# Last layer of a four-layer image kernel: row-by-row copy of the turned banks, one gelu instruction per channel group

## Chip, core and metric

One NeuronCore of one Trainium2 chip runs the whole program. The metric is the device time of one execution in microseconds (us), lower being better. The kernel before took 12187.03 us, the median of three runs (12183.24 to 12192.82).

## The reference, cut to what matters

Four layers run one after the other on x of shape (4, 48, 256, 256), each as x + layer(groupnorm(x)), all in float32. Only the last one is touched:

```python
y = jnp.einsum('oc,bchw->bohw', w_in, x)            # 48 -> 288 channels
yp = y as 8x8 patches
f = jnp.fft.rfft2(yp) * fft_mask[None]
y = irfft2(f), patches put back
y = depthwise 3x3 conv of y, padding 1
x1, x2 = jnp.split(y, 2, axis=1)                    # 144 channels each
g = jax.nn.gelu(x1, approximate=False) * x2
return jnp.einsum('oc,bchw->bohw', w_out, g)        # 144 -> 48 channels
```

## The kernel before, in words

`stage_l3` is the last layer. It works in N = 66 slabs: 33 bands of eight image rows, once for the images 0 and 2 and once for 1 and 3. Every engine has its own instruction stream, written out by hand, and semaphores join them. `n` is the slab, `j` one of three channel groups (24 channels of x1 and the 24 of x2 that belong to them), and `u = 3 n + j` counts the groups.

The steps, with the engine that does each, are these.

- **Mixing** (`channels`, matmul L2255). TensorE multiplies the 32 patch columns with the input weights, in twelve groups: eight of 3 columns and four of 2. Group 0 to 11 go in turn through four pairs of PSUM banks. Of each pair ScalarE (ACT) copies one bank and VectorE (DVE) the other to the tile `y` (`read_y`, L2389 on ACT, L2373 on DVE). From group 4 on, TensorE waits until the group four places ahead has been read by both.
- **Convolution** (`convolve`, matmul L2298). For each channel one matrix takes the 64 pixels of a patch to 10 x 10 places: mask, transforms and 3x3 filter in one. The 24 channels go in five bank groups (5, 5, 5, 5, 4 channels); ACT copies x1 and DVE x2 to the tile `turn` (`read_turn`, L2389 and L2383). `CONV_SLOTS` says which bank pair each group takes.
- **Edges.** The outer ring of the 10 x 10 places belongs to neighbours. SP moves two edge columns by DMA (`move_edges`, L2203), GpSimd (POOL) adds them (L2528), then adds the strip kept from the band above (L2534, it posts `carried`), and keeps a new strip (L2538).
- **Gelu** (ACT, L2396) in place on the x1 part of `turn`, in two halves of four of the eight columns, 768 elements a lane each. **Gate** (`gated`, DVE, L2472): gelu(x1) times x2, in two halves, each behind its own gelu half.
- **Turning** (`transpose`, L2320). TensorE transposes the gated tile into four banks: two behind the first gate half, two behind the second. `TURN_SLOTS` names the banks.
- **Copy of the turned banks** (`read_rows`, ACT, L2389): four copies of 512 elements a lane to the tile `rows`, each once its bank is turned.
- **Projection** (`project`, L2334) with the output weights for all three groups, then DVE adds the residual (`residual`, L2480, it posts `f_out`) and SP stores.

TensorE's order in one slab is: convolution of group 0, turning of group 2 of the slab before, convolution of group 1, projection of the slab before, turning of group 0, convolution of group 2, mixing for the next slab, turning of group 1. Three of its waits matter here. In the convolution of group 2 the bank groups 0 and 1 wait for the second and the fourth residual, and bank group 2 waits for all four copies of the turned banks of group 0. In the convolutions of groups 0 and 1 the fourth bank group waits until ACT and DVE have read the first. `load_x` (SP, L2187) loads the next slab's input once TensorE has finished mixing: 384 KB a half, into the one tile `x`.

ACT and DVE take their work in the order of the code. ACT before, in one slab:

```python
for g in range(COMP):
    read_turn(act, copy, 0, n, 0, g, a_done, a_out)
    if g in (0, 2) and not first:
        gelu(u - 1, g // 2)
...
for g in range(YR):
    read_y(act, copy, 0, n + 1, g, False, a_done, b_done, a_out)
    if g in (3, 6):
        gelu(u + 1, g // 6)
```

DVE has its gate halves at the same places one group later: after groups 1 and 3 of the convolution, and after groups 4 and 7 of the mixing. "The seventh copy" below is DVE's copy of mixing group 6, "the eighth" that of group 7.

Of the kernel before, what the change touches and what calls it, by code (L numbers as in the profile page):

```python
# [13 lines left out]
ACT = mybir.ActivationFunctionType  # L14
# [2081 lines left out]
def stage_l3(nc, D, S):  # L2096

    C3 = 3 * C
    TX, PX = W // 8, 64
    BANDS = H // 8 + 1  # L2100
    N = 2 * BANDS
# [11 lines left out]
    with nc.cleanup_on_exit(), ExitStack() as ctx:  # L2113
        def sb(name, shape):
            return ctx.enter_context(nc.sbuf_tensor(f"l3_{name}", shape, F32))
# [4 lines left out]
        def sem(name):  # L2120
            return nc.alloc_semaphore(f"l3_{name}")
        d = sb("d", [128, C3, PPOS])
        y = sb("y", [128, C3, 2 * TX])
        turn = sb("turn", [128, 2, 10, 10, 2, CH])
# [4 lines left out]
        rows = sb("rows", [128, 3, GROUPS, 2, 2 * TX])  # L2129
# [16 lines left out]
        t_done, t_out, p_done, f_out = sem("t_done"), sem("t_out"), sem("p_done"), sem("f_out")  # L2146
        edged, carried, saved, mixing, blank = (sem(n) for n in ("edged", "carried", "saved", "mixing", "blank"))
        parted, ended_edge = sem("parted"), sem("ended_edge")
        gelu_out, gate_out = sem("gelu_out"), sem("gate_out")
# [6 lines left out]
        def turn_banks(j):  # L2156

            return [bank for slot in TURN_SLOTS[j] for bank in slots[slot]]

        def half(u, part, h):  # L2160

            return turn[:, u % 2, 1:9, 4 * h:4 * h + 4, part, :]

        def gated_half(u, h):

            return gate[:, u % 2, 32 * h:32 * h + 32, 0:CH].rearrange("p (x y) i -> p x y i", y=4)

        def slabs(work):

            for q in range(2):  # L2170
                for ty in range(BANDS):
                    n = q * BANDS + ty
                    work(q, ty, n, n == 0, n == N - 1)
# [192 lines left out]
        def read_y(eng, copy, s, n, g, first, done, other, ready):  # L2366

            if g == 0 and not first:
                eng.wait_ge(other, n * AB)
            eng.wait_ge(done, n * AB + (g + 1))  # L2370
            bank = slots[MIX_SLOTS[g % 4]][s]
            patches = y[:].rearrange("p c (t s) -> p c t s", s=2)[:, :, STARTS[g]:STARTS[g] + SIZES[g], s]
            copy(patches, bank[:, 0:SIZES[g] * C3].rearrange("p (t c) -> p c t", c=C3)).then_inc(ready, 1)  # L2373
# [12 lines left out]
        @block.scalar  # L2386
        def _(act):
            def copy(o, i):
                return nc.scalar.activation(o, i, ACT.Copy)  # L2389

            def gelu(u, h):

                if h == 0:
                    act.wait_ge(edged, u + 1)
                    act.wait_ge(carried, u + 1)
                nc.scalar.activation(half(u, 0, h), half(u, 0, h), ACT.Gelu).then_inc(gelu_out, 1)  # L2396

            def read_rows(n, j):

                u = n * 3 + j  # L2400
                if j == 0 and n > 0:
                    act.wait_ge(p_done, n * 4)
                for i, bank in enumerate(turn_banks(j)):
                    act.wait_ge(t_done, u * 4 + i + 1)
                    copy(rows[:, j, 4 * i:4 * i + 4].rearrange("p q r (s t) -> p (q r) t s", s=2),
                         bank[:].rearrange("p (q t s) -> p q t s", t=TX, s=2)).then_inc(t_out, 1)
            act.wait_ge(blank, 2)
            for g in range(YR):
                read_y(act, copy, 0, 0, g, True, a_done, b_done, a_out)

            def slab(q, ty, n, first, last):
                u = n * 3
                for g in range(COMP):
                    read_turn(act, copy, 0, n, 0, g, a_done, a_out)
                    if g in (0, 2) and not first:
                        gelu(u - 1, g // 2)
                if not first:
                    read_rows(n - 1, 2)
                for g in range(COMP):
                    read_turn(act, copy, 0, n, 1, g, a_done, a_out)  # L2420
                for h in range(2):
                    gelu(u, h)
                read_rows(n, 0)
                for g in range(COMP):
                    read_turn(act, copy, 0, n, 2, g, a_done, a_out)
                if last:
                    for h in range(2):
                        gelu(u + 1, h)
                else:
                    for g in range(YR):  # L2430
                        read_y(act, copy, 0, n + 1, g, False, a_done, b_done, a_out)
                        if g in (3, 6):
                            gelu(u + 1, g // 6)
                read_rows(n, 1)
            slabs(slab)
            for h in range(2):
                gelu(N * 3 - 1, h)
            read_rows(N - 1, 2)

        @block.vector  # L2440
        def _(dve):
            nc.vector.memset(lt, 0.0).then_inc(cleared, 1)
            dve.wait_ge(cleared, 1)
            for q in range(2):
                for s in range(2):
                    b = q + 2 * s
                    nc.vector.tensor_scalar(lt[:, q, s * HI:s * HI + C], S["k_ident"][0:C, 0:C], S["gn"][0:C, b, 0:1], None,
                                            ALU.mult)
                    last = nc.vector.tensor_copy(lt[:, q, s * HI + C:s * HI + C + 1], S["gn"][0:C, b, 1:2])
            last.then_inc(prep, 1)  # L2450
            nc.vector.memset(out[:], 0.0)
            nc.vector.memset(edge[:], 0.0)
            nc.vector.memset(gate[:], 0.0)
            dve.wait_ge(wy_done, 1)
            for q in range(2):
                last = nc.vector.tensor_copy(wy[:, q, :], e[q][0:HI + C + 1, 0:C6])
            last.then_inc(wy_out, 1)
            dve.wait_ge(wy_out, 1)
            for k in range(4):
                last = nc.vector.memset(e[k][32:HI, :], 0.0)  # L2460
            last.then_inc(blank, 1)
            dve.wait_ge(blank, 1)
            dve.sem_inc(blank, 1)
            for g in range(YR):
                read_y(dve, nc.vector.tensor_copy, 1, 0, g, True, b_done, a_done, b_out)

            def gated(u, h):

                dve.wait_ge(gelu_out, u * 2 + h + 1)
                if u >= 2:  # L2470
                    dve.wait_ge(t_done, u * 4 - 6 + 2 * h)
                nc.vector.tensor_tensor(gated_half(u, h), half(u, 0, h), half(u, 1, h), ALU.mult).then_inc(gate_out, 1)  # L2472

            def residual(n, m):

                dve.wait_ge(p_done, n * 4 + m + 1)
                if m == 0:
                    dve.wait_ge(res_loaded, n * 64 + 64)
                o = out[:, m].rearrange("p s (t x) -> p (s t) x", x=8)
                nc.vector.tensor_tensor(o, e[m][0:HI + C, :].rearrange("p (x t) -> p t x", x=8), o, ALU.add)\  # L2480
                    .then_inc(f_out, 1)

            def slab(q, ty, n, first, last):
                u = n * 3
                for g in range(COMP):
                    read_turn(dve, nc.vector.tensor_copy, 1, n, 0, g, b_done, b_out)
                    if g in (1, 3) and not first:
                        gated(u - 1, g // 2)
                for g in range(COMP):
                    read_turn(dve, nc.vector.tensor_copy, 1, n, 1, g, b_done, b_out)  # L2490
                for h in range(2):
                    gated(u, h)
                if not first:
                    for m in range(4):
                        residual(n - 1, m)
                for g in range(COMP):
                    read_turn(dve, nc.vector.tensor_copy, 1, n, 2, g, b_done, b_out)
                if last:
                    for h in range(2):
                        gated(u + 1, h)  # L2500
                else:
                    for g in range(YR):
                        read_y(dve, nc.vector.tensor_copy, 1, n + 1, g, False, b_done, a_done, b_out)
                        if g in (4, 7):
                            gated(u + 1, g // 7)
            slabs(slab)
            for h in range(2):
                gated(N * 3 - 1, h)
            for m in range(4):
                residual(N - 1, m)  # L2510
# [79 lines left out]
```

## Time and profile before

| | |
|---|---|
| median of three runs | 12187.03 us |
| the profiled execution, its own time | 12192.53 us |
| its span, first to last instruction | 12190.5 us |
| mean granted TensorE clock | 0.978 |
| busy in the whole span: PE / DVE / ACT / POOL | 94% / 58% / 45% / 40% |
| last layer | from 9444 us to the end, 66 slabs |
| 9480 to 12150 us (2670 us): PE busy | 2287.07 us |
| the same: ACT, DVE, POOL busy | 2010.65, 1636.81, 1173.94 us |

A slab takes about 40 us. The 2 us between the profiled execution's own time and its span lie ahead of the first and behind the last instruction. A row of a timeline gives start and duration in us; "idle before" is what the engine waited just ahead, and "issue" stands for a wait that no semaphore of the profile explains. Where several neighbouring instructions of a kind are merged, their number follows an x.

### The profile page before, as it was taken

The page shows a single profiled execution, that of the slowest core. Times are in us where ns is not written, and L with a number is a line of the kernel's source. Part 1 is how long each engine was busy: PE and PEld are TensorE (multiplying, and loading weights), DVE is VectorE, ACT ScalarE, POOL GpSimd, SP SyncE. Part 2 cuts the span into 40 slices and gives each one's busy share as a digit, 9 for nine tenths or more (in the row PEclk, how much of TensorE's full clock was granted, in tenths as well). Part 3 has the DMA queues.
Part 4 walks back from the last instruction along what each step waited for, and adds up shares of the span by engine and source line. Part 5 has one row for each costly group of instructions (what it writes and reads, how often), then busy time and mean ns, then how long its engine had stood idle before and what let it go on. Part 6 is the DMA issues. An engine that isn't in the chain of part 4 may idle for free. (4 is left out here: it accounts for less than half of the span.)

```text
span 12190.5 us, 377334 instructions
## 1 busy us (share of the span) xinstructions
PE 11481.4 (94%) x157286; PEld 8021.8 (66%) x157286; DVE 7085.2 (58%) x16108; ACT 5452.4 (45%) x10670; POOL 4928.3 (40%) x4166
## 2 busy tenths in 40 slices
PE   8999999899989999899999999999999888888888
PEld 7877444399977777555555555555555676676776
DVE  0000355544435544688888888888887665666665
ACT  0000111143433333355555555555554777777776
POOL 0000222211430045566666666666665444444444
PEclk9999999999999999899999999999999999999999
DMA  4333466696894488766666666666665443343443
GB/s 141 132 131 134 126 159 157 149 170 103 152 170 146 137 214 229 111 88 88 88 88 88 89 89 87 89 89 87 88 88 81 105 101 91 95 100 94 98 94 88
DMA packets 2340706, 1418.36 MB, mean 116 GB/s; under 512 B 1877404, under 2 KB 2250395, under 8 KB 2253487
## 3 DMA queue, kind: packets, MB, share of 16 engines
q1 hardware_dynamic: 2064428, 1296.69, 53.9%
q10 hardware_dynamic: 275072, 105.14, 3.7%
q8 instruction: 812, 13.30, 0.5%
q14 instruction: 394, 3.23, 0.1%
HBM read 648.90 MB, written 450.45 MB: 90 GB/s over the span
## 5 line engine op out<-in xcount | busy, mean ns | idle before, releaser
L1795 PE MATMUL l_m<-l_wa,l_pix 128*128 128x288 f32 x8192 | 2211.2, 413 | 2.7 <-DVE l_wb L1977 2.7
L1795 PEld LDWEIGHTS l_m<-l_wa,l_pix 128*128 128x128 f32 x8192 | 1475.3, 190 | 688.5 <-issue 361.5
L1651 POOL TENSOR_TENSOR l_qkv<-l_qkv,l_copies 128x576 f32<-128x576 f32 x1024 | 1438.4, 1405 | 630.6 <-DVE l_qkv L1988 617.0
L1641 POOL TENSOR_TENSOR l_pix<-l_raw 128x516 f32<-128x516 f32 x1024 | 1218.6, 1190 | 1042.3 <-DVE l_t L2025 1017.3
L1476 PE MATMUL l1h_ps<-l1h_ring,l1h_w 96*96 96x256 f32 x6120 | 1326.2, 379 | 62.8 <-ACT l1h_ring L1418 59.2
L1476 PEld LDWEIGHTS l1h_ps<-l1h_ring,l1h_w 96*96 96x96 f32 x6120 | 998.4, 163 | 390.4 <-issue 59.4
L1509 DVE SCALAR_TENSOR_TENSOR l1h_ring<-l1h_ps,l1h_bias,l1h_columns 96x256 f32<-96x256 f32 x1020 | 671.1, 658 | 676.3 <-PE l1h_ps L1476 670.6
L509 PE MATMUL l0a_rows<-l0a_x 128*49 128x245 f32 x8144 | 1043.9, 371 | 0.0
L870 PE MATMUL l0b_bank<-l0b_x,l0b_w 49*64 49x512 f32 x9216 | 1001.3, 593 | 4.4 <-DVE l0b_w L896 4.4
L1890 ACT ACTIVATE l_ks<-l_f 94x384 f32<-94x384 f32 x1024 | 498.7, 487 | 838.2 <-PE l_f L1810 838.2
L1810 PE MATMUL l_f<-l_qkv,l_a 64*94 64x384 f32 x4096 | 835.7, 484 | 1.6 <-POOL l_qkv L1651 1.5
L870 PEld LDWEIGHTS l0b_bank<-l0b_x,l0b_w 49*64 49x64 f32 x9216 | 439.2, 133 | 563.6 <-issue 563.6
L1801 PE MATMUL l_m<-l_wb,l_left 58*128 58x288 f32 x4096 | 774.1, 455 | 0.0
L1460 POOL TENSOR_TENSOR l1h_columns<-l1h_blocks,l1h_ring 96x2048 f32<-96x2048 f32 x63 | 350.8, 5590 | 1033.4 <-DVE l1h_ring L1509 1033.4
L1895 ACT ACTIVATE l_sd<-l_mv,l_eps 128x4 f32<-128x4 f32 x512 | 152.2, 297 | 1289.2 <-DVE l_mv L2008 1289.2
L1901 ACT ACTIVATE l_y<-l_i,l_shift,l_rsd 128x96 f32<-128x96 f32 x2048 | 711.1, 427 | 14.2 <-DVE l_shift L2015 0.6
L1224 PE MATMUL l1v_ps<-l1v_ring_w,l1v_w 48*48 48x130 f32 x20480 | 632.0, 272 | 45.4 <-ACT l1v_ring_w L1147 41.2
L509 PEld LDWEIGHTS l0a_rows<-l0a_x 128*49 128x49 f32 x8144 | 601.8, 124 | 107.5 <-issue 1.4
L2298 PE MATMUL l_a<-l_d,l_y 64*64 64x100 f32 x10296 | 570.5, 255 | 89.6 <-ACT l_rows L2389 35.0
L2383 DVE COPY l_turn<-l_b 128x500 f32<-128x500 f32 (+1 forms) x528 | 351.7, 666 | 505.7 <-PE l_b L2298 502.7
L1224 PE MATMUL l1v_ps<-l1v_ring_p,l1v_w 48*48 48x128 f32 x20320 | 615.1, 269 | 7.3 <-issue 6.9
L1224 PEld LDWEIGHTS l1v_ps<-l1v_ring_w,l1v_w 48*48 48x48 f32 x20480 | 586.4, 120 | 48.6 <-issue 48.5
(272 smaller groups left out, 22474.9 us busy)
## 6 DMA issues: line engine op xcount, KB each, us to landing
l0a_x<-x_px_dram SPq DMA_DIRECT2D x128, 1176.0 KB, 5.1
l_edge<-l_turn SPq DMA_DIRECT2D x396, 236.2 KB
l0b_x<-x_in_dram SPq DMA_DIRECT2D x128, 493.8 KB
l_raw<-l_raw SPq DMA_DIRECT2D x128, 483.6 KB, 7.3
l_raw<-x_dram SPq DMA_DIRECT2D x1270, 48.0 KB, 3.7
l_x<-x3p_dram SPq DMA_DIRECT2D x132, 384.0 KB
l_out<-x_dram SPq DMA_DIRECT2D x264, 192.0 KB, 4.4
out_dram<-l_out SPq DMA_DIRECT2D x132, 384.0 KB, 4.6
```

The source lines that it names most:

```text
L509: last = nc.tensor.matmul(o[odd * ODD:odd * ODD + C1, lo:lo + n * C1], x[:, ks, ys, 2 + odd, :], x[:, k, y, e0 + odd:e0 + odd + n, :].rear ...
L870: last = nc.tensor.matmul(bank[2 * n + rt][h * HI:(h + 1) * HI, :], w[part, t, :], rows(part, k, 4 * n + h + t // 3 - rt)[:, :, t % 3:t % ...
L1224: last = nc.tensor.matmul(ps[g][side(c), r, 0:width], w[side(r), t, :], x, start=(t == 0), stop=(t == TAPS - 1), skip_group_check=True)
L1476: last = nc.tensor.matmul(ps[g][0:C2, 0:GI * V], w[:, kernel, s, :], ring[:, g, before % DEEP, :, s:s + V], start=(s == 0), stop=(s == 2))
L1509: nc.vector.scalar_tensor_tensor(out=ring[:, g, x % DEEP, :, 1:V + 1], in0=ps[g][0:C2, 0:GI * V].rearrange("p (i v) -> p i v", i=GI), scal ...
L1641: nc.gpsimd.tensor_tensor(pix[:, n % 2, i, half * HALF:(half + 1) * HALF].rearrange("p (r w) -> p r w", w=PW), in0, in1, op).then_inc(pix_ ...
L1651: nc.gpsimd.tensor_tensor(q, q, copies[:, g % 2, 1:2, :].broadcast_to([128, 2, OUTC]), ALU.add)\
L1795: last = nc.tensor.matmul(bank[i][:, 0:OUTC], pix[:, k, i, first:first + 128], wa[:, b, i, :], start=True, stop=(i in (1, 2)))
L1801: nc.tensor.matmul(bank[i][:, 0:OUTC], left[rows, k, first:first + 128], wb[rows, b, :], start=False, stop=True).then_inc(conv_done, 1)
L1810: last = nc.tensor.matmul(f[0:SLOTS, h, 0:2 * QK].rearrange("p (n o) -> p n o", n=2), a[k, 0:SLOTS], qkv[k, j % 4, 2 * r:2 * r + 2, 0:QK], ...
L1901: last = nc.scalar.activation(y[:, g, m, :], iv[:, m * C2:(m + 1) * C2], ACT.Identity, scale=rsd[:, g, m:m + 1], bias=shift[:, g, m:m + 1])
L2298: last = nc.tensor.matmul(bank[part * 64:(part + 1) * 64, i * PPOS:(i + 1) * PPOS], y[rows_of, c, :], d[rows_of, c, :], start=True, stop=True,
```

## The change

1. `read_rows` copies a turned bank in the order of its destination. Before, the innermost loop took the two values s = 0, 1, which are neighbours in PSUM, and wrote them 32 elements apart. Now the innermost loop takes the 32 values of t, which lie two elements apart in PSUM, and writes them side by side. Source, destination and values are the same.
2. `gelu` does a group's 8 x 8 x 24 elements in one instruction, behind the same two waits, and posts `gelu_out` once. Both gate halves wait for that one.
3. The places: ACT's gelu of group 2 stands after bank group 1 of the next slab's convolution (before: halves after 0 and 2), that of group 1 after mixing group 4 (before: 3 and 6). DVE's gate halves stand after bank groups 2 and 3 (before: 1 and 3), and after mixing groups 6 and 8 (before: 4 and 7). Gelu and gate of group 0 stay where they were.

```diff
             def copy(o, i):
                 return nc.scalar.activation(o, i, ACT.Copy)
 
-            def gelu(u, h):
-
-                if h == 0:
-                    act.wait_ge(edged, u + 1)
-                    act.wait_ge(carried, u + 1)
-                nc.scalar.activation(half(u, 0, h), half(u, 0, h), ACT.Gelu).then_inc(gelu_out, 1)
+            def gelu(u):
+
+                act.wait_ge(edged, u + 1)
+                act.wait_ge(carried, u + 1)
+                kept = turn[:, u % 2, 1:9, 0:8, 0, :]
+                nc.scalar.activation(kept, kept, ACT.Gelu).then_inc(gelu_out, 1)
...
-                    copy(rows[:, j, 4 * i:4 * i + 4].rearrange("p q r (s t) -> p (q r) t s", s=2),
-                         bank[:].rearrange("p (q t s) -> p q t s", t=TX, s=2)).then_inc(t_out, 1)
+                    copy(rows[:, j, 4 * i:4 * i + 4].rearrange("p q r (s t) -> p (q r) s t", s=2),
+                         bank[:].rearrange("p (q t s) -> p q s t", t=TX, s=2)).then_inc(t_out, 1)
...
                     read_turn(act, copy, 0, n, 0, g, a_done, a_out)
-                    if g in (0, 2) and not first:
-                        gelu(u - 1, g // 2)
+                    if g == 1 and not first:
+                        gelu(u - 1)
...
-                for h in range(2):
-                    gelu(u, h)
+                gelu(u)
                 read_rows(n, 0)
...
                 if last:
-                    for h in range(2):
-                        gelu(u + 1, h)
+                    gelu(u + 1)
                 else:
                     for g in range(YR):
                         read_y(act, copy, 0, n + 1, g, False, a_done, b_done, a_out)
-                        if g in (3, 6):
-                            gelu(u + 1, g // 6)
+                        if g == 4:
+                            gelu(u + 1)
                 read_rows(n, 1)
             slabs(slab)
-            for h in range(2):
-                gelu(N * 3 - 1, h)
+            gelu(N * 3 - 1)
             read_rows(N - 1, 2)
...
             def gated(u, h):
 
-                dve.wait_ge(gelu_out, u * 2 + h + 1)
+                dve.wait_ge(gelu_out, u + 1)
...
                     read_turn(dve, nc.vector.tensor_copy, 1, n, 0, g, b_done, b_out)
-                    if g in (1, 3) and not first:
-                        gated(u - 1, g // 2)
+                    if g in (2, 3) and not first:
+                        gated(u - 1, g - 2)
...
                         read_y(dve, nc.vector.tensor_copy, 1, n + 1, g, False, b_done, a_done, b_out)
-                        if g in (4, 7):
-                            gated(u + 1, g // 7)
+                        if g in (6, 8):
+                            gated(u + 1, g // 8)
```

## Rows read from the trace of the kernel before

**Rows 1.** Waits of TensorE, 9480 to 12150 us: total us, times, longest.

```profile
PE l_e L2298 <- issue: 110.6, 48, 4.6
PE l_e L2255 <- issue: 46.3, 46, 2.6
PE l_a L2298 <- ACT l_rows L2389: 34.6, 63, 0.9
PE l_a L2298 <- ACT l_turn L2389: 27.2, 77, 0.5
PE l_e L2320 <- ACT l_y L2389: 26.1, 37, 1.4
...
PE l_a L2320 <- DVE l_gate L2472: 18.4, 30, 1.5
```

**Rows 2.** Chain of waits in one slab, 10940 to 10982 us: start, us, what.

```profile
10944.29 0.85 ACT l_turn L2396
...
10945.17 0.97 DVE l_gate L2472
...
10947.00 2.43 ACT l_rows L2389 x3
...
10949.73 1.16 ACT l_rows L2389
...
10969.93 1.85 issue
```

**Rows 3.** Last layer, groups of instructions kept apart by shape: busy us, mean ns.

```profile
L2396 ACT ACTIVATE l_turn<-l_turn 128x768 f32<-128x768 f32 x396 | 324.3, 835 | 194.9 <-POOL l_turn L2534 192.8 <-POOLq L2531 2.1
...
L2389 ACT ACTIVATE l_rows<-l_b 128x512 f32<-128x512 f32 x264 | 300.6, 1139 | 0.0
...
L2389 ACT ACTIVATE l_turn<-l_a 128x400 f32<-128x400 f32 x66 | 33.3, 505 | 18.4 <-PE l_a L2298 18.3
```

**Rows 4.** The same slab, timeline of TensorE's weight loads: start, us.

```profile
10948.25 0.89 PEld L2298 LDWEIGHTS l_e<-l_d,l_y 64*64 64x64 f32 x40 [0.27 <-DVE l_out L2480]
10949.44 0.89 PEld L2298 LDWEIGHTS l_e<-l_d,l_y 64*64 64x64 f32 x40 [0.30 <-DVE l_out L2480]
10950.93 0.13 PEld L2298 LDWEIGHTS l_a<-l_d,l_y 64*64 64x64 f32 x1 [0.59 <-ACT l_rows L2389]
```

**Rows 5.** Chain of waits in two other slabs: the long wait after a load.

```profile
10885.32 3.70 issue
...
11048.00 4.06 issue
```

**Rows 6.** Timeline of SP: first half of the input load, three slabs.

```profile
10880.47 0.31 SPq L2187 DMA_DIRECT2D l_x<-x3p_dram  x1
...
10963.79 0.31 SPq L2187 DMA_DIRECT2D l_x<-x3p_dram  x1
...
11043.91 0.31 SPq L2187 DMA_DIRECT2D l_x<-x3p_dram  x1
```

**Rows 7.** Timeline of DVE while two slabs are mixed.

```profile
10960.94 0.73 DVE L2373 COPY l_y<-l_b 128x432 f32<-128x432 f32 x1 [0.30 <-PE l_b L2255]
10961.67 0.70 DVE L2373 COPY l_y<-l_e 128x432 f32<-128x432 f32 x1
10962.26 1.32 DVE L2472 TENSOR_TENSOR l_gate<-l_turn 128x768 f32<-128x768 f32 x1
...
10998.35 1.24 DVE L2373 COPY l_y<-l_b 128x432 f32<-128x432 f32 x2
10999.46 0.73 DVE L2373 COPY l_y<-l_e 128x432 f32<-128x432 f32 x1
11000.07 2.71 DVE L2472 TENSOR_TENSOR l_gate<-l_turn 128x768 f32<-128x768 f32 x1
```

**Rows 8.** Timeline of POOL in the same two slabs: the edge add.

```profile
10960.52 2.25 POOL L2528 TENSOR_TENSOR l_turn<-l_turn,l_edge 128x960 f32<-128x960 f32 x1
...
10999.74 2.23 POOL L2528 TENSOR_TENSOR l_turn<-l_turn,l_edge 128x960 f32<-128x960 f32 x1
```

## The prediction

> **What bounds the kernel now.** I read the waits of TensorE in the last layer first. It works for most of a slab, and its idle time falls into two kinds [rows 1]. The first is "issue", a wait that no semaphore explains: 110.6 us in the convolution's e banks alone, 46.3 us in the mixing's. The second is waiting for ACT and for the gate: 34.6 us for the copy of the turned banks, 27.2 us for ACT's copies behind it, 26.1 us for ACT's copies of the mixing, 18.4 us for the gate. Together the second kind is 106 us, 0.9% of the kernel, and it is all that this change can take away from TensorE. So the question is not how much ACT gets faster but which of these waits has nothing behind it.
>
> Then I read the chain of waits through one slab [rows 2]. It runs from POOL's adds to the gelu, the first gate half, the turning, the four copies and back to TensorE: this stretch is bound by ACT and DVE. Later in the slab it runs through a wait of 1.85 us under "issue" that ends at 10971.79. Three such waits end at 10889.02 (10885.32 and 3.70), 10971.78 and 11052.06 (11048.00 and 4.06) [rows 2, 5]. The loads of the next input begin at 10880.47, 10963.79 and 11043.91 [rows 6], so the waits end 8.55, 7.99 and 8.15 us after their load began, although they are 1.85 to 4.06 us long. I take it that TensorE's next instructions arrive behind the load. Whatever TensorE gains between the end of mixing, which starts the load, and this point only makes that wait longer.
>
> **The copies of the turned banks.** 792 of them (12 a slab) take 1139 ns for 512 elements, while 400 elements in runs of four take 505 ns on the same line [rows 3]. The rate between 505 ns at 400 and 835 ns at 768 elements (the gelu) is 0.90 ns an element, which gives 605 ns for 512. The extra half microsecond goes with writing neighbours of the source 32 elements apart, which no other copy here does, and the new order writes side by side. Reading at a stride of two in PSUM has no row of its own; the 400-element copies read at a stride of 100, and cost nothing for it that shows. So a copy is between 605 ns and the present 1139 ns; a lower end is excluded by the rate. I take 610 ns, by the nearest row. ACT gets rid of 792 x 0.53 = 420 us of work. The Trainium skill would have it otherwise: its page "ScalarE: Activation LUTs", section "What ACT_TABLE_LOAD costs", gives an ACTIVATE a fixed part plus 0.833 ns an element and no term for the order. By that alone both orders cost 613 ns, and the 1139 ns of the row contradicts it; read as "order doesn't matter", it is rival 3 below.
>
> **The gelu in one.** One of 768 takes 835 ns, a pair 1.58 us from the first start to the last end. At the rate above one of 1536 takes 835 + 768 x 0.90 = 1525 ns; no row excludes some 50 ns less or more. ACT's work hardly changes. But the first gate half used to start after the first gelu half (10944.29 + 0.85, gate at 10945.17 [rows 2]) and now starts 0.68 us later (1.53 instead of 0.85).
>
> **Group 0, turning to convolution of group 2.** This is the stretch where both edits meet. Everything behind the first gate half moves by 0.68 us: turning, the residuals on DVE, and the bank groups 0 and 1 that wait for them, from 10948.25 and 10949.44 [rows 4] to 10948.93 and 10950.12. Group 1 issues 0.89 us, so group 2 could start at 10951.01. Before, it started at 10950.93, held by the last of four copies that follow each other every 0.92 us (10947.00 to 10950.89 [rows 2]). With copies of 0.61 us behind banks that are turned every 0.44 us, the last ends near 10949.8 and holds nothing. The copies win what the gelu loses: +0.08 us a slab. A small gain is left where the projection ends later than the gate: then TensorE already turns later than it might, and part of the 0.68 us is hidden. The wait for the last copy shows how much: 0.40 us in a slab where the gate bounds, 34.6 / 63 = 0.55 us on average [rows 1], so 0.15 us. Sum: -0.07 us a slab. DVE's residuals come 0.68 us nearer to POOL's edge add of group 1; they have only one operand in SBUF, and I cost that at nothing.
>
> **Turning of group 1, convolution of group 0, behind the load.** Faster copies remove the wait for ACT's copies (part of the 27.2 us), and DVE's new order lets turning start before the second gate half (part of the 26.1 us). Both lie between the load and the wait of 8 us after it, which covers them; a slab without that wait would gain up to 0.6 us, and I see one such in seven, where the later gate (gelu now after bank group 1, gate halves after 2 and 3) takes it back. I cost it at nothing.
>
> **Convolution of group 1 and projection.** The wait for ACT behind the copies of group 2, 0.2 to 0.4 us, goes. But the turning of group 0 that follows is bound by POOL, gelu and gate, so TensorE only waits there instead. Nothing.
>
> **Mixing: what the moved gate does.** Here is the cost. DVE and POOL exclude each other: a gate half issued at 11000.07 into POOL's edge add (10999.74 to 11001.97) took 2.71 us, the add's rest plus 0.8; the one at 10962.26, with 0.51 us of the add left, took 1.32 us [rows 7, 8]; without POOL it takes 0.97 us [rows 2]. The page "SBUF — State Buffer" of the Trainium skill, § "Who interferes with whom", says the same of a DVE instruction with two SBUF inputs against a GpSimd one that reads SBUF; the trace agrees.
>
> Before, this wait struck the second half, behind the eighth copy. What it delayed, turning of group 1, lies behind the load and is covered. Now the first half stands between the seventh and the eighth copy, and the eighth holds mixing group 11, the last, which starts the load. In the slab of 10953 the seventh copy ends at 10961.67, inside the add of 10960.52 to 10962.77. The gate half would run from 10962.77 to 10963.6 and the eighth copy end at 10964.2 instead of 10962.37 [rows 7, 8]. TensorE started its last group near 10962.9 and would start it near 10964.25: 1.34 us lost, on the path. In the slab of 10992 the seventh copy ended at 10999.59 with a gate half ahead of it that now comes behind, so the new one starts near 10999.0, ahead of the add at 10999.74. Then only the longer gelu on ACT costs: three copies queue behind it, and the last group starts about 0.3 us late. Five more slabs from 10832 to 11076 are of these two kinds: two like the first (1.52 us, and 1.58 us that an "issue" wait in the last group covers, so 0) and three like the second (0.35, 0 and 0). The mean of the seven is (1.34 + 1.52 + 0.31 + 0.35) / 7 = 0.50 us a slab. Its bounds are 0, if the gate always gets ahead, and about 1.4 us, if it never does. The gate's own wait for the gelu ends in time in both.
>
> **Sum.** 66 x (0.50 - 0.07) = +28 us. The last slab's end loses 0.6 us by the gelu and wins about as much by the copies. Against the profiled execution's 12192.5 us that is 12220.5 us; the median is 5.5 us lower, so 12215 us. A measurement can tell about 0.2%, 24 us, from no change, so the forecast lies on that line.
>
> **Rivals.**
> 1. The gains reach TensorE (faster). The issue wait would be a fixed length and not a fixed distance from the load. For it: some slabs have none. Against it: the three distances above. Then the 27.2 us and half of the 26.1 us come free, 5 us at group 0, and the gate costs nothing if POOL's add is mostly later: 12187 - 45 = 12142 us.
> 2. The moved gate mostly gets ahead of POOL's add. Gates issued before it are the commoner kind in my sample (four of seven), and 0.3 us of lead decides. Then 66 x (0.15 - 0.07) = +5 us: 12192 us, no change.
> 3. The new order isn't faster, 1139 ns stays. Then group 2 of the convolution goes on waiting for the last copy, and the 0.68 us count whole: 66 x (0.68 - 0.15 + 0.50) = +68 us, 12255 us. Against it: the 400-element row.
> 4. The gate meets the add in nearly every slab: 66 x (1.4 - 0.07) = +88 us, 12275 us. This decides once the seventh copy ends less than a gelu's delay ahead of the add; a slab that starts mixing with an issue wait is already there.
>
> **How the numbers follow.** Forecast 0.41, rival 1 0.18, rival 2 0.24, rival 3 0.06, rival 4 0.11. The forecast's own range is 12200 to 12235 us, by a mean cost of the gate between 0.3 and 0.8 us; a little over half of it is beyond 24 us. So faster 0.18, same 0.24 + 0.17 = 0.41, slower 0.24 + 0.06 + 0.11 = 0.41. The range of 8 in 10 reaches from rival 1 to rival 4, 12142 to 12275 us.
>
> **What would show it.** Copies of the turned banks at about 610 ns and ACT's busy time down by some 450 us, with a span that hardly moves or grows. No wait of TensorE for them, and first bank groups of the convolution of group 2 about 0.7 us later behind POOL's add. Issue waits that still end about 8 us after the load, and are longer. The first gate half in the mixing at 2 to 3 us in some half of the slabs, with TensorE waiting for DVE before its last group. The forecast is wrong if that wait is absent, if the issue waits end earlier after the load, or if the copies stay above 1 us.

## The result, and the profile after

The changed kernel takes 12290.01 us, the median of four runs (12280.23 to 12307.36). The kernel before took 12185.46 us beside it. The ratio is 1.0081, with an interval of 1.0068 to 1.0093: slower by 0.8%, some 99 us. The forecast was 12215 us. Its range ended at 12275, so the result lies outside it, on the side that it gave 0.41 to. The profiled execution took 12280.78 us.

The page of the profile of the changed kernel, its span and busy times:

```profile
span 12278.7 us, 377136 instructions
...
PE 11520.0 (94%) x157286; PEld 8079.5 (66%) x157286; DVE 7120.8 (58%) x16108; ACT 5167.4 (42%) x10472; POOL 4931.7 (40%) x4166
```

The groups of instructions of its last layer, kept apart by shape (busy us, mean ns, idle before):

```profile
L2469 DVE TENSOR_TENSOR l_gate<-l_turn 128x768 f32<-128x768 f32 x396 | 460.8, 1178 | 313.1 <-ACT l_turn L2396 313.0
...
L2396 ACT ACTIVATE l_turn<-l_turn 128x1536 f32<-128x1536 f32 x198 | 291.9, 1474 | 195.6 <-POOL l_turn L2531 195.6
...
L2389 ACT ACTIVATE l_rows<-l_b 128x512 f32<-128x512 f32 x264 | 158.7, 601 | 7.6 <-PE l_b L2320 7.1
```

ACT did what was forecast of it. A copy of a turned bank takes 601 ns instead of 1139 [rows 3] (forecast 610), the long gelu 1474 ns (forecast 1525). ACT is busy for 285 us less, not 450: the forecast added durations, and the records of copies that follow each other overlap. They start every 0.48 us now and every 0.92 before.

Waits of TensorE in the changed kernel, 9480 to 12150 us, as in [rows 1] (total us, times, longest):

```profile
PE l_e L2298 <- issue: 135.7, 52, 5.1
PE l_e L2255 <- issue: 70.2, 65, 3.0
PE l_a L2320 <- DVE l_gate L2469: 60.3, 49, 5.9
PE l_a L2255 <- issue: 36.9, 24, 3.2
PE l_b L2298 <- issue: 33.2, 17, 3.7
PE l_a L2298 <- issue: 29.0, 19, 3.2
PE l_b L2255 <- issue: 24.0, 18, 3.3
PE l_a L2320 <- DVE l_y L2373: 14.9, 26, 1.4
```

The waits for the copies (34.6 us), for ACT's copies behind them (27.2) and for ACT's mixing copies (26.1) [rows 1] are gone. In their place stand the gate (60.3 instead of 18.4 us), DVE's mixing copies (14.9 us) and more "issue" in mixing (70.2 instead of 46.3 in the e banks) and in the convolution (135.7 instead of 110.6).

To see where the time went, 64 whole slabs of each trace were laid out by the starts of TensorE's steps and of the load. (Such figures by slab, here and below, are counted from the kept traces instruction by instruction; no single view of the profile prints them.) Mean us of each stretch:

| | mixing to load | load to turning of group 2 | to turning of group 0 | to next mixing | slab |
|---|---|---|---|---|---|
| before | 10.52 | 10.33 | 12.98 | 7.33 | 41.16 |
| after | 11.60 | 10.56 | 13.53 | 6.71 | 42.41 |
| difference | +1.08 | +0.23 | +0.55 | -0.62 | +1.25 |

66 slabs of 1.25 us are 82 of the 88 us between the two spans. The last two differences are -0.07 us together, as forecast. The first is over twice the forecast 0.50, and the second was to be 0.

One slab of the changed kernel shows most of it. Its timeline of DVE ahead of the store (group 0's gate halves and the residuals), that of SP with store and load, and TensorE's waits (the instruction behind each, in brackets the idle time before it):

```profile
11008.22 1.83 DVE L2469 TENSOR_TENSOR l_gate<-l_turn 128x768 f32<-128x768 f32 x2 [4.47 <-ACT l_turn L2396]
11009.96 2.48 DVE L2477 TENSOR_TENSOR l_out<-l_e,l_out 112x512 f32<-112x512 f32 x4
```

```profile
11012.47 0.79 SPq L2209 DMA_DIRECT2D out_dram<-l_out  x2
...
11029.27 0.31 SPq L2187 DMA_DIRECT2D l_x<-x3p_dram  x1
```

```profile
11019.29 0.34 PE L2255 MATMUL l_b<-l_wy,l_x 49*64 49x144 f32 x2 [2.08 <-issue]
11028.43 0.72 PE L2255 MATMUL l_e<-l_wy,l_x 49*64 49x144 f32 x16 [0.88 <-issue]
11037.13 0.24 PE L2298 MATMUL l_b<-l_d,l_y 64*64 64x100 f32 x1 [2.83 <-issue]
```

The gate waits 4.47 us for the gelu, the residuals end at 11012.44 and the store is issued at 11012.47: a later gelu is a later store. The last of the three waits ends 7.86 us after the load, as the forecast had it. But there is a wait of 2.08 us of the same kind early in mixing, and it ends 6.82 us after the store of line 2209. The distance is no exact constant: over all slabs such early waits end 5 to 8.5 us after the store, 6.9 us on average. Its slab's clock, in stretches (us, busy time and instructions of PE, PEld, DVE, ACT, POOL, granted clock, DMA share, GB/s):

```profile
11015.80:11020.70 4.90, 2.82 (x95) 2.54 (x88) 2.29 (x4) 2.40 (x5) 1.59 (x3) 1.00 0.60 177
11020.70:11024.10 3.40, 3.40 (x67) 3.40 (x63) 1.97 (x4) 2.25 (x4) 1.80 (x2) 0.50 1.00 196
11024.10:11029.20 5.10, 4.22 (x124) 3.78 (x117) 4.65 (x7) 3.71 (x8) 4.09 (x3) 1.00 0.05 12
...
11037.80:11041.20 3.40, 3.40 (x40) 3.16 (x33) 2.03 (x3) 1.97 (x4) 0.49 (x1) 0.50 0.02 5
```

Behind each of the two long waits TensorE's granted clock is 0.50, 1.2 instead of 2.4 GHz, for 3.4 us. In the mixing TensorE gets through 67 matmuls in 3.40 busy us at half clock and through 124 in 4.22 behind it. Last, DVE and POOL in the same mixing:

```profile
11024.64 1.48 DVE L2373 COPY l_y<-l_b 128x432 f32<-128x432 f32 x2 [0.41 <-PE l_b L2255]
11025.99 1.76 DVE L2469 TENSOR_TENSOR l_gate<-l_turn 128x768 f32<-128x768 f32 x1
11027.68 0.98 DVE L2373 COPY l_y<-l_e 128x432 f32<-128x432 f32 x2
```

```profile
11022.79 2.24 POOL L2525 TENSOR_TENSOR l_turn<-l_turn,l_edge 128x960 f32<-128x960 f32 x1
11025.11 1.83 POOL L2531 TENSOR_TENSOR l_turn<-l_turn,l_strip 128x768 f32<-128x768 f32 x1
```

The first gate half stands between the seventh and the eighth copy and is caught by POOL's strip add, which ends at 11026.94. The gate ends at 11027.75, the add's rest plus 0.81 us, and TensorE's last mixing group starts at 11028.43 after 0.88 us of waiting. The profile files this wait under "issue", though it ends about when the eighth copy does, the first of the two that start at 11027.68. Laid out over all slabs, the last group starts within 0.15 us of the eighth copy's end in 65% of them (8% before), and the first gate half takes 1.65 us on average (1.05 before).

### The profile page after: what moved, and what is told of

It reads as the page before. It is cut to its first block and busy times, and to the rows that moved or that the text cites. A ratio compares the mean times of both kernels' runs of the same rounds, so it can differ in the third digit from the quotient of the medians.

```text
span 12278.7 us, 377136 instructions
## 1 busy us (share of the span) xinstructions
PE 11520.0 (94%) x157286; PEld 8079.5 (66%) x157286; DVE 7120.8 (58%) x16108; ACT 5167.4 (42%) x10472; POOL 4931.7 (40%) x4166
## 5 line engine op out<-in xcount | busy, mean ns | idle before, releaser
L2298 PE MATMUL l_e<-l_d,l_y 64*64 64x100 f32 x17424 | 508.7, 259 | 151.0 <-issue 143.8
L2469 DVE TENSOR_TENSOR l_gate<-l_turn 128x768 f32<-128x768 f32 x396 | 460.8, 1178 | 313.1 <-ACT l_turn L2396 313.0
```

Source lines behind the costliest of these rows:

```text
L2298: last = nc.tensor.matmul(bank[part * 64:(part + 1) * 64, i * PPOS:(i + 1) * PPOS], y[rows_of, c, :], d[rows_of, c, :], start=True, stop=True,
```

## The experiments

Three theories stand against each other at first. **M2** is the forecast's cost: the gate half between the seventh and eighth copy. **M1** says that the one gelu of group 0 is the cost, since what the copies win behind it is given back elsewhere. A third, **B**, says that ACT's long gelu in the mixing holds TensorE by its own queue. The expectations, written down before each run, call M1 and M2 together "Theory A" in the runs on the gelu and the gate. Ratios are to the kernel before, run beside each kernel, with 95% intervals.

**The copy order alone**, on the kernel before (`e1_copy_only`):

```diff
-                    copy(rows[:, j, 4 * i:4 * i + 4].rearrange("p q r (s t) -> p (q r) t s", s=2),
-                         bank[:].rearrange("p (q t s) -> p q t s", t=TX, s=2)).then_inc(t_out, 1)
+                    copy(rows[:, j, 4 * i:4 * i + 4].rearrange("p q r (s t) -> p (q r) s t", s=2),
+                         bank[:].rearrange("p (q t s) -> p q s t", t=TX, s=2)).then_inc(t_out, 1)
```

> The kernel before with the new copy order alone; gelu in halves and all places as before. Theory A (two causes: the one gelu of group 0 delays gate, residuals and with them the store behind which TensorE's instructions for the early mixing arrive; and the moved gate half waits for POOL's edge add ahead of the eighth copy of the mixing): neither cause is in this kernel, the copies take 0.60 us, the waits for them (34.6 us before) go, and the early-mixing issue waits grow by most of it, so 12187 - 15 = about 12172 us (12150 to 12190). Theory C (the faster copies themselves harm, by reading PSUM in another order beside TensorE): slower than 12210 us. If all waits for ACT reached the end: 12187 - 62 = 12125 us.

Measured: 0.9995 [0.9985, 1.0006], no change, though ACT is rid of the work. Waits of TensorE in it, 9480 to 12150 us:

```profile
PE l_e L2298 <- issue: 119.3, 49, 4.9
PE l_e L2255 <- issue: 49.8, 46, 2.6
PE l_a L2255 <- issue: 38.0, 30, 3.5
...
PE l_a L2320 <- DVE l_gate L2472: 26.7, 36, 2.2
```

The stretch up to mixing is 0.79 us shorter a slab (6.54 instead of 7.33), the forecast's 0.6 us for the copies or a little more. Mixing to load is 0.64 us longer (11.16 instead of 10.52), though nothing in the mixing was changed. So this is where the win is given back. TensorE's "issue" waits in the mixing grow from 1.46 to 1.75 us a slab, and its time at half clock there from 0.48 to 1.19 us. By these figures an estimate is 0.29 us of longer waiting and up to 0.36 us (half of 0.71) of slower clock. The 0.64 us also accounts for as much of the 1.08 us above.

**The two undone one at a time.** DVE's gate halves in the changed kernel behind mixing groups 8 and 9, where no copy that a later mixing group waits for stands behind them (`e3_gates_8_9`):

```diff
-                        if g in (6, 8):
-                            gated(u + 1, g // 8)
+                        if g in (8, 9):
+                            gated(u + 1, g - 8)
```

> The changed kernel with DVE's two gate halves of group 1 after mixing groups 8 and 9 instead of 6 and 8, so that the eighth copy has no gate ahead of it. Theory A: the wait of TensorE ahead of the last mixing group goes, the turning of group 1 starts later but is covered by the issue wait behind the load, and the time falls by 0.5 to 0.9 us a slab: 12290 - 45 = about 12245 us (12230 to 12260). Theory B (the loss comes from ACT, whose gelu of 1.47 us holds its mixing copies back): no change, about 12290 us.

Measured: 1.0058 [1.0042, 1.0075]. And the changed kernel with group 0's gelu in two halves again, each gate half behind its own (`e4_halves_group0`):

```diff
-                nc.scalar.activation(kept, kept, ACT.Gelu).then_inc(gelu_out, 1)
+                if u % 3 == 0:
+                    for h in range(2):
+                        nc.scalar.activation(half(u, 0, h), half(u, 0, h), ACT.Gelu).then_inc(gelu_out, 1)
+                else:
+                    nc.scalar.activation(kept, kept, ACT.Gelu).then_inc(gelu_out, 2)
...
-                dve.wait_ge(gelu_out, u + 1)
+                dve.wait_ge(gelu_out, u * 2 + (h + 1 if u % 3 == 0 else 2))
```

> The changed kernel with the gelu of group 0 alone in two halves again; groups 1 and 2 in one instruction, places as changed. Theory A: the first gate half of group 0 starts 0.63 us earlier behind POOL's add, residuals, store and the early-mixing issue waits with it, so 0.4 to 0.6 us a slab: 12290 - 33 = about 12257 us (12245 to 12270), and the wait of TensorE for the gate ahead of the turning of group 0 falls from 0.85 to about 0.3 us a slab. Theory B: no change beyond 10 us.

Measured: 1.0037 [1.0023, 1.0051]. The wait of TensorE for the gate in `e4_halves_group0`, 60.3 us in the changed kernel:

```profile
PE l_a L2320 <- DVE l_gate L2473: 25.4, 38, 1.4
```

The one gelu of group 0 costs 0.44%, the gate's place 0.23%. Only the first difference is clear of its intervals; the gate's is some 28 us where 45 were expected. Both theories seem to hold a part, M1 the larger.

**DVE's places alone**, on the kernel before (`e5_places_only`):

```diff
-                    if g in (1, 3) and not first:
-                        gated(u - 1, g // 2)
+                    if g in (2, 3) and not first:
+                        gated(u - 1, g - 2)
...
-                        if g in (4, 7):
-                            gated(u + 1, g // 7)
+                        if g in (6, 8):
+                            gated(u + 1, g // 8)
```

> The kernel before with only DVE's gate halves moved (after bank groups 2 and 3, and after mixing groups 6 and 8); gelu in halves, old copies, ACT untouched. Theory A: the moved gate half meets POOL's edge add ahead of the eighth copy, so 0.5 to 0.9 us a slab more: 12187 + 45 = about 12232 us (12215 to 12250), with gate halves of 1.5 to 3 us ahead of the eighth copy. Theory B (ACT's long gelu): no change, about 12187 us.

Measured: 1.003 [1.0019, 1.0041], some 37 us. Mixing to load grows from 10.52 to 11.02 us, by the forecast's 0.50, and the last mixing group is held by the eighth copy in 56% of the slabs. But the edit moves group 2's gate halves too, and the stretch from the load to the turning of group 2 grows by another 0.35 us (10.68 instead of 10.33), which the forecast had at nothing. TensorE's waits show it, where before had none for DVE's mixing copies:

```profile
PE l_a L2320 <- DVE l_y L2373: 21.8, 37, 1.8
...
PE l_e L2255 <- DVE l_y L2373: 19.2, 15, 2.1
```

**Both undone** (`e6_halves0_gates_8_9`, the two diffs of `e3_gates_8_9` and `e4_halves_group0` together):

> The changed kernel with both suspects undone: gelu of group 0 in two halves, and the gate halves of group 1 after mixing groups 8 and 9. Theory A with the two causes adding up: 12290 - 53 - 28 = about 12209 us, between 12195 and 12225. Theory B (what is left is ACT's long gelu in the mixing, behind which TensorE still waits before mixing group 9): it stays 10 to 25 us above the kernel with the new copies alone (about 12186 us). Were one cause all of it, this run would equal the better of the two single ones, about 12237 us.

Measured: 1.0019 [1.0009, 1.003]. The two parts add up: 0.44 + 0.23 = 0.67 against 0.62 taken back. Here the gate's part shows in the trace: mixing to load takes 10.98 us, against 11.61 in `e4_halves_group0`, which differs only by the gate's place. What is left is slower than `e1_copy_only` by 0.24%. The difference between the two is the single gelu of groups 1 and 2 and where the gates behind it stand.

**Group 1's gelu in halves too**, on `e6_halves0_gates_8_9` (`e9_halves_groups_0_1`):

```diff
...
-                        if g == 4:
-                            gelu(u + 1)
+                        if g in (3, 6):
+                            gelu(u + 1, g // 6)
```

> The kernel with both suspects undone (1.0019 of before), and the gelu of group 1 in two halves at its old places on ACT as well; only group 2 is left in one instruction. Theory B (ACT's gelu of 1.47 us holds mixing group 5's copy, and TensorE waits for it ahead of group 9 in half the slabs): 15 to 30 us less than that run, about the kernel with the new copies alone (ratio 0.998 to 1.000). Otherwise, if what is left comes from the gate halves after mixing groups 8 and 9 or from group 2's places: the ratio stays at 1.002.

Measured: 1.0009 [1.0, 1.0019], the intervals of the two touch. In `e6_halves0_gates_8_9` mixing group 9 starts as ACT's copy of group 5, queued behind the long gelu, ends in 52% of the slabs; here in none. B is seen in the trace; these runs put it at about 0.1%, a difference that isn't clear of their intervals.

**Where the copies' win goes: the load.** A load of an eighth of the input after slab 0, on the kernel before (`d0_small_load`) and with the new copy order (`d1_small_load_copy`):

```diff
-                    sp.dma_start(x[s * HI:s * HI + C].rearrange("p t x -> p (t x)"), src.rearrange("a c n -> (a c) n"))\
-                      .then_inc(x_loaded, 16)
+                    piece = slice(0, TX * PX if first else TX * PX // 8)
+                    sp.dma_start(x[s * HI:s * HI + C].rearrange("p t x -> p (t x)")[:, piece],
+                                 src.rearrange("a c n -> (a c) n")[:, piece]).then_inc(x_loaded, 16)
```

> The kernel before, but the input loads of all slabs after the first move only an eighth of their columns (the mixing goes on with the rest as it was; results are not the reference's). Theory A (TensorE's instructions arrive behind the load): the issue waits in the convolution of group 0, 2.1 us a slab, go or fall below 0.5 us, with them most of the stretches at half clock behind them (1.8 us a slab), and the time falls by 1.5 to 3 us a slab: 12187 - 150 = about 12040 us (11980 to 12090). Rival D (the wait has a cause of its own and only happens to stand 8 us behind the load): no change, the waits stay where they are, within 30 us of 12187.

> The same small loads with the new copy order alone. In the kernel with full loads this edit changed the time by -0.05%. Theory A (what the copies give is covered by issue waits, and what is left is lost to the half clock that follows longer waits): with the cover behind the load gone, the copies are worth 0.3 to 0.8 us a slab more than before, so 20 to 50 us less than the run with small loads and old copies. Theory C (the faster copies are worth nothing by themselves): the two runs with small loads agree within 10 us.

Measured: 0.9909 [0.9893, 0.9926] and 0.9856 [0.984, 0.9873]. Waits of TensorE in the convolution's e banks of `d0_small_load` (110.6 us before):

```profile
PE l_e L2299 <- issue: 19.1, 23, 1.8
```

The wait behind the load goes with the load's size: in the convolution of group 0 it falls from 2.12 to 0.12 us a slab. And without that cover the same edit that was worth nothing is worth 12079.62 - 12017.03 = 63 us. Most of that win lies behind the load, 0.66 us a slab up to the turning of group 0. Of the 0.56 us that the copies save ahead of mixing, 0.35 us is again given back in it (mixing to load 11.17 us instead of 10.82).

**The same for the store.** Store and residual load an eighth after slab 0, on the kernel before (`d2_small_store`):

```diff
-                    sp.dma_start(D["out"][n, side], out[side * HI:side * HI + C].rearrange("p y s w -> p (y s w)"))\
+                    piece = slice(0, 8 * W if n == 0 else W)
+                    sp.dma_start(D["out"][n, side][:, piece], out[side * HI:side * HI + C].rearrange("p y s w -> p (y s w)")[:, piece])\
...
+                        width = W if first else W // 8
...
```

> The kernel before, but the store and the residual load of every slab after the first move an eighth of their data (most of the output is left unwritten and most of the residual stands still). Theory A (the issue waits early in the mixing end about 6.5 us after the store was issued, because TensorE's instructions come behind it): the early waits, 0.64 us a slab, and most of the late ones go, the mixing's start-to-load falls from 10.5 to about 9.3 us, and the time falls to 12187 - 80 = about 12107 us (12060 to 12140); the waits behind the input load stay. Rival D (those waits have a cause of their own): no change within 20 us.

Measured: 0.9943 [0.9922, 0.9963]. Waits of TensorE in it, those of the mixing and the first of the convolution:

```profile
PE l_e L2300 <- issue: 122.1, 40, 5.4
...
PE l_e L2257 <- issue: 6.6, 12, 1.3
```

"Issue" in the mixing's e banks falls from 46.3 to 6.6 us, and the waits early in mixing from 0.64 to 0.01 us a slab; the one behind the load stays. Mixing to load takes 8.80 us. The run cuts the residual load too, but in the slab shown above that is issued at 11018.64, when the wait had begun 1.4 us before. The run says less of the waits late in mixing: they stand 3 us and more behind the residual load, end 10 to 16 us after the store, and could hang on either. The early waits keep their distance from the store on average: counted from its second half, which is issued 0.38 us after the first, they end 6.5 us after it before, 6.5 in the changed kernel and 6.4 in `e1_copy_only`. From the start of mixing they end 2.7, 3.4 and 3.4 us after it, so they follow the store and not the mixing. What TensorE waits for, no view of the profile names; that it is its next instructions, as the forecast took it, no run here tests.

**A smaller load at a time.** The second half of the input load, with the new copy order, behind the edge moves of group 0 (`e7_split_load_copy`) or of group 1 (`e10_split_later_copy`), and the latter with the whole change (`e11_split_later_after`):

```diff
-                for s in range(2):
+                for s in halves:
...
+                    load_x(*after, (0,))
...
+                if not last:
+                    load_x(*after, (1,))
```

> The new copies alone, with gelu and places as before, and the input load split: the images 0 and 1 half is issued where it was, the other half only behind the edge move of channel group 0, some 11 us later; the slab needs it 25 us later. Theory A: the load takes half as long, the issue waits in the convolution of group 0 end about 4 us earlier and fall below 0.7 us a slab, some of it comes back where the second half runs, and the time falls to 12186 - 80 = about 12105 us (12040 to 12150), below both kernels. Rival D: no change within 20 us.

> The new copies alone with the split load, whose second half is now issued behind the edge moves of channel group 1 instead of group 0. In the run with the second half behind group 0 (ratio 0.9973) the stretch from the turning of group 2 to that of group 0 was 1.3 us a slab longer than without the split, since POOL waits there for edges that now share the queue. Theory A: that 1.3 us comes back and about 0.3 us is lost to the store behind the second half, so the ratio falls to about 0.992 (0.989 to 0.996), some 12095 us. If the second half costs the same wherever it stands: 0.997.

> The changed kernel as a whole with the same late split load. Theory A: with less cover behind the load the gelu and the moved gate cost as much or more and the copies give more; the whole change still costs, so this run is 60 to 110 us above the new copies alone with the same split. If the change only lost by the longer issue waits and the half clock behind them: within 30 us of it.

Measured: 0.9973 [0.9963, 0.9982], 0.9885 [0.9862, 0.9907] and 0.9972 [0.9962, 0.9982]. SP's timeline and TensorE's waits in `e10_split_later_copy`:

```profile
10939.36 0.31 SPq L2187 DMA_DIRECT2D l_x<-x3p_dram  x1
...
10963.38 0.55 SPq L2187 DMA_DIRECT2D l_x<-x3p_dram  x1
...
10966.04 0.79 SPq L2209 DMA_DIRECT2D out_dram<-l_out  x2
...
10979.98 0.31 SPq L2187 DMA_DIRECT2D l_x<-x3p_dram  x1
```

```profile
PE l_e L2301 <- issue: 58.9, 47, 2.8
...
PE l_e L2258 <- issue: 35.0, 37, 2.0
```

The first half is issued at 10939.36, the second at 10963.38, ahead of the store, and the last line is the next slab's first half. Over all slabs the second half comes 19 to 24 us after the first. Behind a half load the waits in the convolution of group 0 end 6.0 us after it, in both kernels with the new copies alone. In `e7_split_load_copy` the stretch from the turning of group 2 to that of group 0 takes 14.26 us instead of 12.94 in `e1_copy_only`, in `e10_split_later_copy` 13.20: behind group 0's edges the second half gives half of what is won behind the load back. The longest wait in the convolution's e banks of `e10_split_later_copy` is 2.8 us instead of 4.9 in `e1_copy_only`, and all of them together 58.9 instead of 119.3 us. At 12066.0 us this kernel beats both, the one before by 1.15%. With the whole change it takes 12160.35 us, 94 us more. Both kernels have the new copies, so 94 us is the price of the rest of the change, gelu and places. Without the split the same difference, from `e1_copy_only` to the changed kernel, is 104 us, 0.8 to 0.9% in both.

**The clock** in these runs, 9480 to 12150 us (to 12000 in the last, which ends earlier; the granted clock is the third number from the end). The changed kernel:

```profile
9480.00:12150.00 2670.00, 2249.78 (x61472) 1870.71 (x61478) 1623.36 (x2327) 1688.08 (x2646) 1148.44 (x940) 0.95 0.39 93
```

`e10_split_later_copy`:

```profile
9480.00:12000.00 2520.00, 2223.65 (x62785) 1849.37 (x62781) 1608.76 (x2381) 1702.22 (x2893) 1162.46 (x960) 0.98 0.41 101
```

Before it was 0.97. Counted one by one, the last layer has 48 stretches at half clock before (194.5 us), 71 in the changed kernel (318.2), 69 in `e1_copy_only` (287.8), 36 in `e10_split_later_copy` (148.0) and 30 in `e11_split_later_after` (122.8). In `e1_copy_only` the slabs that are at full clock throughout take 38.83 us, against 39.64 before: 0.81 us less, about what the copies should bring. But there are 14 of them instead of 27, and they are the slabs that happened to have no long wait, so the comparison is only a hint.

## Why the prediction was wrong, step by step

- **What bounds the kernel.** Right for the load: the waits end 8.0 to 8.3 us after it on average in every kernel that loads as before, 6.0 us after half a load, and `d0_small_load` shows that they come with the load. Incomplete for the rest. The "issue" waits of the mixing, 46.3 us in the e banks [rows 1], were read and then never placed. The early ones follow the store as the others follow the load.
- **The copies.** Right in size (601 ns for 610). The Trainium skill's page "ScalarE: Activation LUTs" (section "What ACT_TABLE_LOAD costs") has a fixed part and 0.833 ns an element, from which an estimate is 613 ns for either order; the new order agrees, the old one at 1139 ns does not.
- **Group 0, "The copies win what the gelu loses: +0.08 us a slab".** This is the step that failed. The stretch itself came out as summed, +0.55 - 0.62 = -0.07 us. But the sum stopped where mixing begins. From the start of the turning of group 0 to mixing group 5 it takes 12.04 us before, 12.04 in `e1_copy_only`, 12.05 in the changed kernel and 12.07 in `e4_halves_group0`: whatever the copies win ahead of mixing is gone by then, in longer waits and in time at half clock. The store's issue follows the gate and DVE's residuals, and not the copies of the turned banks. So the copies' 0.60 us counted nothing, as the forecast had rightly said of a gain ahead of the load. The gelu's delay moves the store and counts whole. In the changed kernel the store's second half comes 3.28 us ahead of mixing instead of 3.97.
- **Mixing, the moved gate, 0.50 us.** Right in mechanism and, in its own stretch, in size: alone it made mixing to load 0.50 us longer, with the last group held by the eighth copy in 56% of the slabs. That the kernel with the places alone is slower by 37 us, against 33 summed, is partly luck, as its trace has 0.35 us a slab more behind the load. In the slab shown it met POOL's strip add instead of the edge add of [rows 8], at the same price. That is again what is said of a DVE instruction with two SBUF inputs beside a GpSimd one that reads SBUF by the Trainium skill's page "SBUF — State Buffer", § "Who interferes with whom".
- **Turning of group 1 and convolution of group 0 at nothing.** Right that the gain is covered (`e1_copy_only`, `d1_small_load_copy`). But the stretch grew by 0.23 us, 15 us in all, which no term held. It also grew by 0.18 us with the new copies alone and by 0.35 us with DVE's places alone; which of the two edits makes the 0.23 us is open.
- **Not in the forecast at all**: ACT's queue in the mixing (about 0.1%, not clear), and the granted clock.
- **The sum put right.** 66 x (0.50 + 0.68 - 0.15) = 68 us with the copies' win struck out, and 15 us for the stretch behind the load: 83 of the 88 us between the spans. The total fits better than its parts: undone one at a time, the gelu gave 0.44% (54 us) and the gate 0.23% (28 us), and with both undone 0.19% was left, of which these runs place some 0.1% with the gelu of group 1, not clear of the intervals. Rival 4 named 12275 us, near the result, but by a gate that meets the add in nearly every slab, and it is 65%. Rival 2 is out by the same 65% and by a first gate half of 1.65 us on average. Rival 1 fell with the load's cover. Rival 3 has the right price by accident: copies that bring nothing because they are slow, where they bring nothing because their win is given back in the mixing.

What stays open is how much of this the clock does. The longer waits have half-clock stretches behind them, and these make the next steps later. No run here changes the clock alone. `e11_split_later_after` bounds it from one side: with 30 such stretches, fewer than before, gelu and places still cost 94 us against `e10_split_later_copy` with 36. So most of their price is in the order of the work. The copies' lost win is, by the estimate above, the clock's about as much as the waits'. The direct test, the new copy order together with the small store, was not run.

## What to carry to other kernels

Sum a change not up to the next step but up to the next wait that keeps its distance from some DMA, and place every "issue" wait of the profile that way before pricing anything: ask of each gain and each delay which DMA it moves. Here a gain that did not bring that DMA forward was given back, while a delay of the DMA counted whole, so that two terms which cancelled in the stretch did not cancel in the kernel. And where one instruction replaces two halves, what waits for the first half pays, even when the engine itself is faster.

## What the runs showed that was not expected

- Two kinds of TensorE's waits without a semaphore end at a distance from the issue of a transfer that changes little from kernel to kernel: on average 8.0 to 8.3 us after the input load (384 KB a half), 6.0 us after half of it, and some 6.5 us after the store, with most single ones within 2 us of that. Both nearly vanish when that transfer is cut to an eighth (the store's together with the residual load), and a load in two halves, the second 19 to 24 us behind the first, is worth 1.1% with the new copy order (ratios 0.9885 and 0.9995 to the kernel before). Where the second half is put matters: behind group 0's edges it is worth 0.2%.
- In the slab shown the granted clock is 0.50 for 3.4 us, beginning 0.7 and 1.4 us after the end of such waits. A kernel with a few more long waits had 71 such stretches instead of 48.
- An ACT copy of 512 elements from PSUM takes 1139 ns when it writes neighbours 32 elements apart, and 601 ns when it writes side by side and reads at a stride of two.
- A gate half caught by either of POOL's adds ends 0.8 us after it, in the three slabs shown, here and in [rows 7, 8].
